# Edge rounds of a graph layer: the third gather moved ahead of the edge rows, a shift ahead of the masks, and the parts of the node products made earlier

## The reference, cut to what matters

```python
h = x @ W
alpha = softmax(where(H.T > 0, leaky_relu(h @ a_node), NEG))     # edge over its nodes
agg = einsum('ben,bnf->bef', alpha, h)                            # one row per hyperedge
beta = sigmoid((h @ a_gn)[:, None, :] + (agg @ a_ge)[:, :, None])
all_he = beta[..., None] * h[:, None] + (1 - beta[..., None]) * agg[:, :, None]
all_he = elu(all_he)
industry = einsum('nm,bmf->bnf', adj / deg, x @ W_ind)
se = tanh(elu(agg) @ fcW + fcb) @ av
coefs1 = softmax(where(H > 0, se[:, None, :], NEG))
g = einsum('bne,benf->bnf', coefs1, all_he)
```

## Time and profile before

| | |
|---|---|
| median of 3 runs | 725.89 us (724.87 to 726.29) |
| profiled execution, its time | 726.31 us |
| its span, first to last instruction | 724.1 us |
| mean granted TensorE clock | 0.970 of 2.4 GHz |
| busy share of the span | PE 92%, DVE 58%, ACT 47%, POOL 40% |
| chain that ended last | PE 53%, POOL 8%, DVE 6%, ACT 4% |

### The profile page before, as it was taken

The page is one execution under the profiler, slowest core; times in us unless marked ns, Lnnn a source line. Parts: engine busy times, 40 slices in busy tenths (PEclk is TensorE's granted clock), DMA queues, the critical chain, the costliest instruction groups (busy, mean ns, idle before and its releaser), DMA issues.

```text
span 724.1 us, 9828 instructions
## 1 busy us (share of the span) xinstructions
PE 668.4 (92%) x3420; PEld 462.6 (64%) x3428; DVE 422.0 (58%) x966; ACT 340.6 (47%) x655; POOL 289.9 (40%) x267
## 2 busy tenths in 40 slices
PE   6898989788799989999999999999999999999993
PEld 2796766566566867633333348887777777778883
DVE  1675656767539852366878756314565767651166
ACT  0861234544366651265666643323446556455214
POOL 0270104565536720010324256122667676760045
PEclk9999999999989699999999999999999999999998
DMA  9120030000000027000100000000000000000013
GB/s 326 38 88 2 1 116 1 1 0 1 1 2 1 4 52 164 19 0 1 37 22 1 1 0 1 1 1 1 2 1 1 0 1 1 1 1 2 1 29 87
DMA packets 14995, 18.34 MB, mean 25 GB/s; under 512 B 10128, under 2 KB 10128, under 8 KB 14944
## 3 DMA queue, kind: packets, MB, share of 16 engines
q1 hardware_dynamic: 14432, 16.06, 7.7%
q10 hardware_dynamic: 512, 1.60, 0.6%
HBM read 11.37 MB, written 2.10 MB: 19 GB/s over the span
## 4 chain that ended last, share of the span: by engine, by line
PE 53%; POOL 8%; DVE 6%; ACT 4%; issue 2%; ACTq 0%; POOLq 0%; DVEq 0%
PE PS L1504 9%; PE PS L1391 7%; PE PS L1374 7%; PE PS L1517 5%; POOL LN_Y L163 4%; PE PS L1557 4%; PE PS L1546 4%; PE PS L182 2%; PE PS L1483 2%; PE PS L1490 2%; PE PS L189 2%; PE PS L1567 2%; DVE arena L2143 2%; DVE LN_ST L140 1%; PE PS L1420 1%
## 5 line engine op out<-in xcount | busy, mean ns | idle before, releaser
L2143 DVE SCALAR_TENSOR_TENSOR arena<-PS,WT,arena 128x256 f32<-128x256 f32 x160 | 77.5, 484 | 49.2 <-PE PS L1517 27.0
L1714 ACT ACTIVATE arena<-PS,spare 128x1024 f32<-128x1024 f32 x64 | 70.8, 1109 | 49.8 <-DVE spare L2080 49.6
L2080 DVE TENSOR_REDUCE spare<-PS 128x1 f32<-128x1024 f32 x64 | 75.6, 1219 | 23.8 <-PE PS L1374 23.7
L1504 PE MATMUL PS<-WH,KK 128*128 128x512 f32 x256 | 86.1, 402 | 0.1
L163 POOL TENSOR_TENSOR LN_Y<-LN_V,CN 128x16 f32<-128x16 f32 (+1 forms) x18 | 50.0, 2779 | 67.6 <-DVE LN_V L155 67.6
L1782 ACT ACTIVATE spare<-PS,WT 128x256 f32<-128x256 f32 x96 | 38.8, 471 | 63.7 <-DVE arena L2143 61.8
L1875 POOL TENSOR_TENSOR arena<-arena,spare 128x128 f32<-128x128 f32 x32 | 13.8, 433 | 134.2 <-DVE spare L2086 123.6
L1391 PE MATMUL PS<-arena 128*64 128x512 f32 x256 | 62.0, 605 | 1.5 <-POOL arena L1875 1.4
L1504 PEld LDWEIGHTS PS<-WH,KK 128*128 128x128 f32 x256 | 48.0, 187 | 16.7 <-issue 5.7
L1504 PE MATMUL PS<-WL,KK 128*128 128x512 f32 x128 | 50.0, 391 | 0.0
L1374 PE MATMUL PS<-arena 64*128 64x512 f32 x192 | 48.2, 617 | 1.4 <-ACT arena L1714 1.4
(11 more groups left out here) (293 smaller groups left out, 1496.8 us busy)
## 6 DMA issues: line engine op xcount, KB each, us to landing
arena<-in_adj_tr SPq DMA_DIRECT2D x8, 512.0 KB, 5.9
arena<-in_x_tr SPq DMA_DIRECT2D x4, 512.0 KB, 8.0
arena<-in_x_nat SPq DMA_DIRECT2D x1, 2048.0 KB, 9.0
arena<-arena SPq DMA_DIRECT2D x7, 256.0 KB, 2.8
arena<-arena SPq DMA_DIRECT2D x12, 128.0 KB, 2.3
spare<-in_w SPq DMA_DIRECT2D x2, 512.0 KB, 4.0
out<-arena SPq DMA_DIRECT2D x4, 256.0 KB, 3.1
out<-arena SPq DMA_DIRECT2D x8, 128.0 KB, 2.2
```

The costliest lines, as they stand in the source:

```text
L1504: ins = pe.matmul(acc, x[:, t % 2, b, :], w[:, k, c], start=(first and n == 0), stop=(not first and n == 2), skip_group_check=True)
L1714: act.activation(EF[2 * (i % RING) + par], banks("S", 2 * i + par).rearrange("p a c -> p (a c)"), ACT.Exp, bias=NMX[:, i, par:par + 1], ac ...
L2080: dve.tensor_reduce(NMX[:, i, par:par + 1], banks("S", 2 * i + par), AX.XY, ALU.max, negate=True).then_inc(max_ready, 1)
L2143: dve.scalar_tensor_tensor(acc, PS[:, four_banks(t, j), d * F:(d + 1) * F], WT[:, e:e + 1], acc, ALU.mult, ALU.add).then_inc(acc_step, 1)
```

## The change

Three edits. On PE, `gather(t, C_)` with its wait for the first shift now stands ahead of `edge_rows(t_next)` with its wait for the masks. On DVE, `shift(A_)` now follows `mix(A_)` directly and `from_first` comes behind it. And all eight `high(t)` and `low(t)` are made beside the industry products: on ACT behind the two tanh and ahead of `industry_out(1)`, on POOL right behind the adjacency's low parts; the rounds hold none of them any more, and PE waits once for all eight instead of at each tile.

```diff
--- before.py
+++ after.py
@@ -362,8 +362,8 @@
                     pool.wait_ge(hph_ready, t + 1)
                     pool.tensor_tensor(HPL[:, t, :], HP[:, t, :], bits(HPH[:, t, :]), ALU.subtract).then_inc(hpl_ready, 1)
 
-                low(0)
-                low(1)
+                for t in range(NT):
+                    low(t)
                 first = first_rounds(pool)
                 for t in range(NT):
                     with pool.Fori(first[t], first[t + 1]) as j:
@@ -376,8 +376,6 @@
                             pool.wait_ge(t_ready, CHUNKS * j + (c + 1))
                             pool.tensor_tensor(groups(S1[:, c, :]), groups(S1[:, c, :]), spread(CC[:, c, :]),
                                                ALU.mult).then_inc(w_ready, 1)
-                    if t + 2 < NT:
-                        low(t + 2)
                     if t >= 1:
                         pool.wait_ge(rn_ready, t)
                         pool.tensor_tensor(groups(GN[:, t - 1, :]), groups(GN[:, t - 1, :]), spread(ZS[:, t - 1, :]),
@@ -483,14 +481,17 @@
                 for par in range(2):
                     act.activation(THE[:, par:BP:2, :], PS[:, 6 + par, 2 * P:4 * P].rearrange("p (a c) -> p a c", c=P), ACT.Tanh,
                                    bias=wt(W_FCB, 1)).then_inc(the_done, 1)
+
+                def high(t):
+                    act.activation(HPH[:, t, :], HP[:, t, :], ACT.Copy).then_inc(hph_ready, 1)
+
+                for t in range(NT):
+                    high(t)
                 industry_out(1)
                 act.wait_ge(seB_ready, 1)
                 act.activation(SEB[:, :, :], PS[:, 4, :].rearrange("p (b e) -> p b e", e=E), ACT.Copy).then_inc(seB_out, 1)
                 industry_out(2)
 
-                def high(t):
-                    act.activation(HPH[:, t, :], HP[:, t, :], ACT.Copy).then_inc(hph_ready, 1)
-
                 def edges_out(dst, done):
                     act.activation(dst[:, :, :], PS[:, 6, 0:ROUND].rearrange("p (c n) -> p c n", n=P), ACT.Copy).then_inc(done, 1)
 
@@ -508,12 +509,10 @@
 
                 act.wait_ge(fold_ready, 1)
                 act.activation(AGS[:, :], PS[:, 7, :], ACT.Copy).then_inc(agh_ready, 1)
-                high(0)
                 first = first_rounds(act)
                 industry_out(3)
                 act.wait_ge(agl_ready, 1)
                 act.activation(AGM1[:, :], bits(AGS[:, :]), ACT.Copy, scale=-1.0).then_inc(agn_ready, 1)
-                high(1)
                 industry_out(4)
                 industry_out(5)
                 act.wait_ge(sT_ready, 1)
@@ -553,8 +552,6 @@
                         act.wait_ge(lg_ready, j + 2)
                         act.wait_ge(cc_ready, j + 1)
                         likely()
-                    if t + 2 < NT:
-                        high(t + 2)
                     act.wait_ge(acc_done, first[t + 1] + 1)
                     act.activation(GN[:, t, :], PS[:, 4, :], ACT.Copy)
                     act.activation(ZS[:, t, :], PS[:, 7, ZN_AT:ZN_AT + B], ACT.Copy).then_inc(acc_out, 1)
@@ -744,10 +741,10 @@
                         dve.wait_ge(be_ready, j + 1)
                         mix(B_, 1)
                         mix(A_, 2)
+                        shift(A_, 2)
                         dve.wait_ge(selg_ready, j + 1)
                         dve.wait_ge(nt_ready, j + 1)
                         from_first(at).then_inc(ns_half, 1)
-                        shift(A_, 2)
                         dve.wait_ge(ns_half, j + 2)
                         to_last(at).then_inc(ns_ready, 1)
                         shift(B_, 1)
@@ -965,7 +962,7 @@
                 industry(7)
                 pe.wait_ge(ind_out, NT)
                 pe.wait_ge(agn_ready, 1)
-                pe.wait_ge(hpl_ready, 1)
+                pe.wait_ge(hpl_ready, NT)
                 pe.wait_ge(nsg_ready, 1)
                 pe.wait_ge(selg_ready, 1)
                 gather(0, B_)
@@ -979,7 +976,6 @@
                         pe.wait_ge(acc_out, t)
                     pe.matmul(PS[:, 4, :], zero16[:, 0:P], zero16[:, :], start=True, stop=False, skip_group_check=True)
                     pe.matmul(PS[:, 7, ZN_AT:ZN_AT + B], zero16[:, 0:P], zero16[:, 0:B], start=True, stop=False, skip_group_check=True)
-                    pe.wait_ge(hpl_ready, min(t + 2, NT))
                     with pe.Fori(first[t], first[t + 1]) as j:
                         k_next, t_next = next_round(j, t, first)
 
@@ -987,10 +983,10 @@
                             pe.wait_ge(w_ready, CHUNKS * j + (c + 1))
                             return pe.matmul(PS[:, 4, :], NST[:, c, :], S1[:, c, :], start=False, stop=True, skip_group_check=True)
 
+                        pe.wait_ge(z_ready, CHUNKS * j + 1)
+                        gather(t, C_)
                         pe.wait_ge(ns_ready, j + 2)
                         edge_rows(t_next)
-                        pe.wait_ge(z_ready, CHUNKS * j + 1)
-                        gather(t, C_)
                         pe.wait_ge(nst_out, j + 1)
                         pe.wait_ge(est_ready, j + 2)
                         turn_edges()
```

## The result

The changed kernel takes 730.11 us (median of 20 runs, 724.15 to 730.92), the kernel before 725.93 in the same series (20 runs, 724.48 to 727.20). The ratio, which goes by the means, is 1.0042, 95% interval 1.0028 to 1.0056: slower by 0.4%, while the medians lie 4.2 us apart. The forecast was 727.5 us, 1.6 above before.

A forecast was written before the change was run, and what follows sets the result against it. PE, DVE and PE again form the round's loop of 11.14 us, with PE waiting for masks. Rounds +0.1 and setup +1.5 make +1.6 us on the median of 725.89: 727.5 us, range 723.6 to 731.0.

The forecast's parts named there:

- the +1.5 of the setup: Ahead of the rounds: POOL's eight early differences delay DVE's chain, net +1.5 us on PE, range 0 to +1.5.
- The middle term: In each round, end of zero products to `turn_edges`: 3.23 us against 2.80, +0.43 in a round like 2.
- the loop's entry: In each round, PE's entry into the gather's loop behind the zero products: taken as 0.12 us.
- the lower bound of 2.98: Least middle term, if the gather hides its last pitch and the loop's entry: 2.98 us, +0.18 a round.
- The masks: DVE in round 2: masks ready between 127.9 and 128.6 us, worth nothing because the gather holds the edge rows longer.
- Round 0: First round, with no `acc_out` to wait for: 1.3 us gained at full clock, 0.7 with the slowest masks.
- The half-clock stretches: PE in the rounds: full clock throughout taken as likelier; if the low stretches stay, the rounds' +0.1 us becomes +3.7.
- the first rival: Low-clock stretches in the rounds stay: +5.2 us if all, +2.8 with one, 728.7 to 731 us; chance 0.20.
- `kq`: Setup: PE's wait for `kq`, whose input `kst` starts with POOL's first difference; taken as 0, up to 1.25 us more.
- DVE's chain from 72 us: Setup: DVE's two-operand operations leading to `edges(0)` meet POOL's last differences, late by 0.2 to 2.7 us.
- the stall at 87.06: Setup: a DVE operation slowed beside POOL's difference there cost 1.06 us, which the change was credited with removing.
- The lock: Setup: DVE operations with two SBUF inputs and POOL's exclude each other for a whole instruction; supports the +1.5 us.

The follow-up runs named there:

- e11: e10 with the changed kernel's PE order (gather ahead of the edge rows) and four zero products behind the edge rows; 721.92 us, ratio 0.9942 to the kernel before.
- e3: The changed kernel with PE's order alone put back (edge rows ahead of the gather); 725.76 us, ratio 1.0002 to the kernel before.
- e10: e8 with POOL's last three differences held until the first masks and zero products ahead of each tile's wait for `acc_out`; 717.68 us, ratio 0.9884.
- e1: The kernel before with only the two reorderings on PE and DVE, highs and lows left in place; 723.76 us, ratio 0.9993.
- e5: The changed kernel with four products of zeros on PE behind the edge rows in every round; 724.63 us, ratio 0.9984 to the kernel before.
- e2: The changed kernel with PE's and DVE's orders both put back, so only highs and lows moved; 725.61 us, ratio 1.0002 to the kernel before.
- e4: The changed kernel with POOL's first difference waiting until DVE's `kq` is there; 728.08 us, ratio 1.0028 to the kernel before.
- e8: e7 with eight more products of zeros on PE ahead of round 0; 722.84 us, ratio 0.9965 to the kernel before.
- e6: The changed kernel with eight products of zeros in PE's wait for `kq`; 726.93 us, ratio 1.0003 to the kernel before.
- e7: The changed kernel with PE's old order, POOL's differences behind `kq` and eight zero products in PE's wait for `kq`; 724.34 us, ratio 0.9985.
- e12: e10 with DVE's old order (first half of the masks ahead of shift A); 718.86 us, ratio 0.9898 to the kernel before.

## Why the prediction was right

The direction was forecast, and about half the size: +1.6 us, where the ratio of 1.0042 makes +3.0 us (2.0 to 4.1 by its interval). The waits in the rounds are as written. That the sum came out so near is in good part luck: two sizes in the rounds were wrong in opposite directions, and the +1.5 of the setup stands for a cost that the profiled execution doesn't have, while the one that it has was set at 0. Point by point:

- **The middle term** was taken as 3.23 us and is 2.84, the same in rounds 1 to 7 and in e11. The mechanism is as written: the gather behind the zero products, then 2 us of edge rows and `edges` with PE idle 1.19. Mis-sized were the loop's entry (taken 0.12; the gather starts 0.14 before the zero products' end) and the chain behind (2.07, measured 1.96). It lies below the lower bound of 2.98, but that bound was added up wrongly: without the gather's last pitch (0.26) and the entry (0.12), 3.23 leaves 2.85. At equal clock a round like round 2 lost 0.05 us (11.19 against 11.14), where +0.43 was forecast.
- **The masks** came 2.55 us behind the start of mix A, where 2.75 to 3.45 was forecast, and that was worth nothing in the changed kernel, as said. The removal of the lows from the rounds is what pays with PE's old order: e3 and e10, rounds of 10.6. That the old order would then gain was not said.
- **Round 0** at full clock was forecast at 10.4 us and is 10.6 in e1 and e5.
- **The half-clock stretches** were taken to vanish, and in rounds 1 to 7 they did. In round 0 one grew to nine microseconds or more. That is the first rival's mechanism, in one place instead of three. It costs 4.8 us (15.38 against e5's 10.61), where the forecast put the three of before at 3.6 together; so the clock in the rounds is 1.1 us worse than before instead of 3.6 better. The step that failed is the judgment that two short idle stretches are better than a long one, which held in rounds 1 to 7 and not in round 0: e5, which fills the last of round 0's, takes the stretch away.
- **The setup** was taken as +1.5 us for DVE's chain from 72 us and 0 for `kq`, with 1.25 as its bound. It was +2.12 the other way round: `kst` lost 1.06 (1.29 instead of 0.23), half clock behind the longer wait the rest, DVE's chain nothing. The tie at 64.64 us went to POOL. Counted from `kst`, the setup is 2.2 us longer than before in the changed kernel and 2.1 in e3, but 1.2 in e2 and e5, where half clock ended sooner. e4 and e8 show that the chain's cost was real (1.27 and 2.71 us of PE's wait) and only covered. The 1.06 us credited for the stall at 87.06 were worth nothing: from DVE's first operation of the chain to mix A it is 30.80 us before and 30.75 without that stall. What kept the cost of e4's chain at 1.27 of 2.6 is slack between it and PE.
- **The lock.** Each DVE operation of 128x512 on two SBUF operands that was held up ends 0.55 us behind the end of a POOL operation that it met (e4: 73.56, 75.26 and 76.96, POOL's ends at 73.01, 74.71 and 76.41), and POOL's operations between them last 1.7 us instead of 1.3. The exclusive lock of the Trainium skill ("SBUF — State Buffer", section "SBUF: two separate sides") fits these. `kst` reads one operand only from SBUF, so the rule for two inputs, which the prediction quotes, does not cover it; that it too was held, to 0.03 us behind POOL's end, is shown by its row and by e4, and the reason for it by no run.

What stays open: why the clock falls where it does, and why some executions of one and the same program get the stretch of round 0 and some don't (e1: four of twelve). The runs show that filling PE's waits makes it rare. A rival that no run tests by itself is that the zeros help by moving what follows. Against it, the kernels that move things but leave round 0's waits open (e1 to e4, e6, e7) spread over 3.7 to 6.6 us, those with zeros there (e5, e8 to e12, 39 executions) over 0.5 to 1.7 us, and e8 over 3.2. Behind the rounds the changed kernel's clock between 220 and 262 us was 0.80 against 0.84, part of the 0.8 us there; that too is unexplained.

## What to carry to other kernels

A block of ready work in a queue is worth what stands behind it: before, the gather filled the wait for another engine's answer; put ahead of the question, it delays the question and leaves the wait empty (0.5 to 0.6 us a round, e11 against e10). Work moved to an idle engine is free only if that engine shares nothing with the one on the path, down to an operation of 22 elements in each of 8 partitions. And where a kernel's times fall in groups with different granted clocks, measure edits with the waits filled; the small differences then show, and here the cheap products of zeros in the waits were themselves worth keeping. Compare at equal clock: the kernel before and e1 look 2.5 us apart only because their clocks differ.

## What the hardware showed beside

- A DVE operation of 8x22 elements took 1.29 us instead of 0.23 because it started 0.01 us behind a POOL operation; in e4, where POOL starts later, it took 0.23. DVE's reductions of one operand were not held: in the trace of before six of them started within POOL's differences of the adjacency (36 to 50 us) and took 1.21 to 1.22 us, as long as the one at 52.37 with POOL idle.
- Half clock lasted 9 us in round 0 of the changed kernel and 14 in e2's although PE was busy at 99% of either stretch; ahead of the first it had idled 0.96, 0.39 and 1.20 us between 105.4 and 110.0, ahead of e2's 2.45 us:

```profile
107.00:121.00 14.00, 13.85 (x41) 10.42 (x42) 5.70 (x13) 3.40 (x8) 3.13 (x3) 0.51 0.13 51
```
- With four zero products (1.03 us in the trace) in a wait of 1.2 that stretch was gone from the profile, and none of 11 executions took over 725.6 us.
